# A graph network on one core: rows turned by transposing DMAs in the batch norm stage, and the middle attention stage's transfers cut by subtile

## The chip, the cores and the metric

The kernel runs on 1 core of one Trainium2 chip. The metric is the device time of one execution in microseconds (us). TensorE multiplies, VectorE, ScalarE and GpSimd do the elementwise work, and SyncE issues most DMAs; the engines meet only at semaphores.

## The reference

Four graph layers stand one behind the other, each with a residual and a layer norm, on 10,000 nodes with 512 features and 5,000 edges:

```
x = layernorm(x + L0(x))   # GIN: two products with W1, W2
x = layernorm(x + L1(x))   # SAGE: two products, batch norm, relu, + x
x = layernorm(x + L2(x))   # GAT twice (4 heads of 256), then a product with Wfc
x = layernorm(x + L3(x))   # GCN: product, batch norm, gelu, + x
```

What matters here: the last step of layer 1, `relu((h - mu) * rsqrt(var + eps) * gamma + beta) + x`, then `layernorm(x + ...)`, then the first product of layer 2, `x @ W1` (512 to 1024 columns), with 8 more columns for the attention logits. And the middle of layer 2: the output of the first attention, relu, times `W2` (1024 to 1024, with 8 logit columns).

## The kernel before, in words

The nodes are padded to 20 groups of 512 (G = 20; GROUP), each of 4 subtiles of 128 rows (S = 4). In the code a group g is named by its pair i and its parity u, g = 2i + u; most buffers are double, by parity. The layers are cut into stages, run one after the other; at a stage's end all engines meet. Within a stage each engine has its own program, in an order that is written out by hand, and waits on semaphores. `in_pairs` runs a body over all groups, `following(i, u)` is the next group, `ahead(i, G)` says that a pair i + 1 exists. Two stages are touched.

Products. fp32 values are split into a high and a low fp16 part, and each product is three fp16 matmuls per chunk of 128 (`split_product`, lines 324 to 326). The rows' parts are the stationary operand, so they are needed with the features on the partitions: turned against the row layout in which norms are computed. 1032 output columns are worked in three thirds of 344.

Batch norm stage (`batch_norm_stage`, from line 1886, "sage"). SyncE loads h (features on partitions) and x (rows on partitions), 1 MB each per group (lines 1937, 1941). ScalarE applies scale, shift and relu to h (2036). TensorE turns h into rows with fp32 transposes against an identity, 4 per subtile (`turn_rows`, 2080). VectorE adds 2x (`residual`, 1997) and takes statistics (1432, 1435), GpSimd the power (1441, 1444), VectorE normalises into b_o (`finish`, 1452). TensorE turns b_o back (`turn_back`, 2090), 4 chunks of 4 transposes into two PSUM banks; ScalarE takes the high parts from PSUM (2042) and VectorE the low parts (2011). Then come the products, 12 of 12 matmuls for a group (`products`), ScalarE copies each third to b_wide (2057), SyncE stores 516 KB per subtile to h1 (1958). GpSimd adds a bias to b_o (1973), SyncE stores it (1948). Everything for group g+1 is worked while TensorE is at the products of g: its group is two blocks of eight transposes for turn_rows and two for turn_back, set between the products.

Middle attention stage (`gat_middle_stage`, from line 2130). For each subtile SyncE loads rows of h1 (512 KB, line 2182), GpSimd gathers sums (1463), VectorE mixes both into t_z (2250) and adds a bias (2255), ScalarE takes relu (2268) and casts the high part t_row_hi (2271), GpSimd the low part t_row_lo (2224). Here the rows are turned by DMAs, not by TensorE: `turn(g)` on SyncE issues one transposing DMA of 128x4096 fp16 for the high parts of a whole group (2190) and one for the low parts (2193), each after all four subtiles are there. Both go through single row buffers, which are free for group g+1 when the transfers of g have landed. TensorE does 288 matmuls per group, ScalarE copies the thirds (2282), SyncE stores (2198).

All the DMAs of SyncE go through one queue, in the order of its program; the first stage of the kernel turns rows by DMA as well (1518, 1521), 128x2048 at a time.

Of the kernel before, what the change touches and what calls it, by code (L numbers as in the profile page):

```python
# [11 lines left out]
ds = bass.ds  # L12
# [118 lines left out]
def in_pairs(eng, n, body):  # L131

    if n > 2:
        with eng.Fori(0, n // 2 - 1) as i:
            for u in range(2):
                body(i, u, False)
    body(n // 2 - 1, 0, False)
    body(n // 2 - 1, 1, True)
# [1750 lines left out]
def batch_norm_stage(kn, layer):  # L1889
# [17 lines left out]
    if sage:  # L1907
        z_hi = kn.buffer(mem, "b_z_hi", [P, 2, 4, D], F16)
        z_lo = kn.buffer(mem, "b_z_lo", [P, 2, 4, D], F16)
        wide = two("b_wide", [P, GAT_ROW], F32)  # L1910
    norm = Norm(kn, mem)

    tp = [[kn.bank[n] for n in (0, 1, 0, 1)]] * 2 if sage else [kn.bank[0:4], kn.bank[4:8]]
    tq = [kn.bank[2], kn.bank[3]]
# [10 lines left out]
    turned = pair("turned", 4 * H if sage else 0)  # L1925
    hi_done = take("hi_done", 4 * G if sage else 0)
    lo_done = take("lo_done", 4 * G if sage else 0)
    prod = take("prod", THIRDS * S * G if sage else 0)
    wide_done = take("wide_done", THIRDS * S * G if sage else 0)
    wide_stored = pair("wide_stored", 16 * 2 * G if sage else 0)  # L1930

    def sync(sp):
        def load(i, u):

            sp.wait_ge(rows_turned[u].sem, rows_turned[u].at(i * S))
            settle(sp, kn)
            sp.dma_start(h[u][:], dram["h"][:, :, ds(i * (2 * GROUP) + u * GROUP, GROUP)]
                         .rearrange("m p n -> p m n")).then_inc(h_in[u].sem, 16)

            sp.wait_ge(y_done[u].sem, y_done[u].at(i * S))  # L1940
            sp.dma_start(x[u][:], node_rows(x_dram, i, u)).then_inc(x_in[u].sem, 16)

        def store(i, u):
            if sage:
                sp.wait_ge(biased[u].sem, biased[u].at(i + 1))
            else:
                sp.wait_ge(rows_out[u].sem, rows_out[u].at(i * S + S))
            sp.dma_start(node_rows(out_dram, i, u), o[u][:]).then_inc(stored[u].sem, 16)

        def group(i, u, last):  # L1950
            g = i * 2 + u
            if ahead(i, G):
                load(i + 1, u)
            store(i, u)
            if sage:
                for s in range(S):
                    sp.wait_ge(wide_done.sem, wide_done.at((g * S + s + 1) * THIRDS))
                    sp.dma_start(dram["h1"][ds(i * (2 * GROUP) + u * GROUP + s * P, P), :], wide[s % 2][:])\
                        .then_inc(wide_stored[s % 2].sem, 16)

        load(0, 0)
        load(0, 1)
        in_pairs(sp, G, group)
        for u in range(2):
            sp.wait_ge(stored[u].sem, stored[u].at(16 * H))
            if sage:
                sp.wait_ge(wide_stored[u].sem, wide_stored[u].at(16 * 2 * G))

    def gpsimd(pool):
        def bias(i, u):  # L1970

            pool.wait_ge(turned[u].sem, turned[u].at(i * 4 + 4))
            nc.gpsimd.tensor_tensor(o[u][:], o[u][:], kn.fc_b[:].unsqueeze(1).broadcast_to([P, S, D]), ALU.add)\
                .then_inc(biased[u].sem, 1)

        def group(i, u, last):
            if not last:
                norm.pool(pool, *following(i, u))
                bias(*following(i, u))

        if sage:
            norm.pool(pool, 0, 0)
            bias(0, 0)
# [4 lines left out]
    def vector(dve):  # L1988
# [18 lines left out]
        def low_parts(i, u):  # L2007
            g = i * 2 + u
            for k in range(4):
                dve.wait_ge(hi_done.sem, hi_done.at(g * 4 + k + 1))  # L2010
                v.scalar_tensor_tensor(out=z_lo[:, u, k, :], in0=tq[k % 2][:], scalar=A_SCALE, in1=z_hi[:, u, k, :],
                                       op0=ALU.mult, op1=ALU.subtract).then_inc(lo_done.sem, 1)

        def group(i, u, last):
            if not last:
                residual(*following(i, u), range(S))
                finish(*following(i, u))
                low_parts(*following(i, u))
# [7 lines left out]
        residual(0, 0, range(S))  # L2026
        if sage:
            finish(0, 0)
            low_parts(0, 0)
        in_pairs(dve, G, group if sage else group_alone)  # L2030

    def scalar(act):
# [6 lines left out]
        def high_parts(i, u, chunks=range(4)):  # L2039
            for k in chunks:  # L2040
                act.wait_ge(turned[u].sem, turned[u].at(i * 4 + k + 1))
                act.activation(z_hi[:, u, k, :], tq[k % 2][:], ACT.Copy, scale=A_SCALE).then_inc(hi_done.sem, 1)

        def group(i, u, last):
            g = i * 2 + u
            for s in range(S):

                if s == 1 and ahead(i, G):
                    apply(i + 1, u)

                w = wide_stored[s % 2]
                act.wait_ge(w.sem, w.at(g * 32 + (s // 2) * 16))
                for n in range(THIRDS):
                    if (s, n) in ((2, 2), (3, 1)) and not last:
                        high_parts(*following(i, u), (0, 1) if s == 2 else (2, 3))
                    act.wait_ge(prod.sem, prod.at((g * S + s) * THIRDS + n + 1))
                    act.activation(wide[s % 2][:, n * THIRD:(n + 1) * THIRD], mm[n], ACT.Copy, scale=UNSCALE)\
                       .then_inc(wide_done.sem, 1)

        if sage:  # L2060
# [3 lines left out]
            in_pairs(act, G, group)  # L2064
# [3 lines left out]
    def tensor(pe):  # L2068
        def turn_rows(i, u, subtiles):
            pe.wait_ge(f_done[u].sem, f_done[u].at(i * 4 + 4))  # L2070
            for s in subtiles:

                if not sage:
                    pe.wait_ge(y_done[u].sem, y_done[u].at((i - 1) * S + s + 1))
                elif s >= 2:
                    pe.wait_ge(y_done[u].sem, y_done[u].at(i * S + s - 1))
                else:
                    pe.wait_ge(y_done[1 - u].sem, y_done[1 - u].at((i + u) * S))
# [4 lines left out]
        def turn_back(i, u, chunks=range(4)):  # L2083
            g = i * 2 + u
            pe.wait_ge(rows_out[u].sem, rows_out[u].at(i * S + S))
            for k in chunks:

                pe.wait_ge(lo_done.sem, lo_done.at(g * 4 + (k - 1 if k >= 2 else 0)))
                for s in range(S):
                    ins = pe.transpose(tq[k % 2][:, s * P:(s + 1) * P], o[u][:, s, k * P:(k + 1) * P], kn.ident[:])  # L2090
                ins.then_inc(turned[u].sem, 1)

        def products(i, u, s, thirds=range(THIRDS)):
            g = i * 2 + u
            parts = lambda k: (z_hi[:, u, k, s * P:(s + 1) * P], z_lo[:, u, k, s * P:(s + 1) * P])
            for n in thirds:
# [6 lines left out]
        def group(i, u, last):  # L2103
            pe.wait_ge(lo_done.sem, lo_done.at((i * 2 + u) * 4 + 4))
            if not last:
                turn_rows(*following(i, u), (0, 1))
            products(i, u, 0)
            if not last:
                turn_rows(*following(i, u), (2, 3))
            products(i, u, 1)  # L2110
            products(i, u, 2, (0, 1))
            if not last:
                turn_back(*following(i, u), (0, 1))
            products(i, u, 2, (2,))
            products(i, u, 3, (0,))
            if not last:
                turn_back(*following(i, u), (2, 3))
            products(i, u, 3, (1, 2))

        if sage:  # L2120
            turn_rows(0, 0, range(S))
            turn_back(0, 0)
# [8 lines left out]
def gat_middle_stage(kn):  # L2131
# [39 lines left out]
    turned_in = pair("turned_in", 32 * H)  # L2171
# [4 lines left out]
    def sync(sp):  # L2176
        def load_rows(g):
            for s in range(S):
                if g:
                    i, u = divmod(g - 1, 2)  # L2180
                    sp.wait_ge(z_mixed.sem, z_mixed.at((g - 1) * S + s + 1))
                sp.dma_start(hrow[:, s, :], dram["h1"][g * GROUP + s * P:g * GROUP + (s + 1) * P, LOGITS:])\
                    .then_inc(h_in[s].sem, 16)

        def turn(g):
            i, u = divmod(g, 2)
            if g >= 2:
                sp.wait_ge(prod.sem, prod.at((g - 1) * S * THIRDS))
            sp.wait_ge(hi_done.sem, hi_done.at(g * S + S))
            sp.dma_start(r_hi[u][:], row_hi[:].rearrange("p s c -> p (s c)"), transpose=True)\  # L2190
                .then_inc(turned_in[u].sem, 16)
            sp.wait_ge(lo_done.sem, lo_done.at(g * S + S))
            sp.dma_start(r_lo[u], row_lo[:].rearrange("p s c -> p (s c)"), transpose=True)\
                .then_inc(turned_in[u].sem, 16)
# [5 lines left out]

        load_rows(0)
        load_rows(1)
        turn(0)
        load_rows(2)
# [11 lines left out]
    def gpsimd(pool):  # L2216

        def low_parts(g):
            i, u = divmod(g, 2)
            if g:  # L2220
                pool.wait_ge(turned_in[1 - u].sem, turned_in[1 - u].at((i + u) * 32))
            for s in range(S):
                pool.wait_ge(hi_done.sem, hi_done.at(g * S + s + 1))
# [39 lines left out]
    def scalar(act):  # L2263
        def parts(i, u, s):
# [4 lines left out]
            act.wait_ge(turned_in[1 - u].sem, turned_in[1 - u].at((i + u) * 32))  # L2269
# [23 lines left out]
    def tensor(pe):  # L2293
        def group(i, u, last):
            g = i * 2 + u
            pe.wait_ge(turned_in[u].sem, turned_in[u].at(i * 32 + 32))
            for s in range(S):
                for third in range(THIRDS):
# [608 lines left out]
```

## Time and profile before

| | |
|---|---|
| median of 3 runs | 4138.68 us (4137.36 to 4145.64) |
| the profiled execution | 4137.12 us, span 4135.1 us |
| TensorE busy | 3554.7 us, 86% |
| VectorE, ScalarE, GpSimd busy | 2089.7, 1479.1, 1476.6 us |
| DMA | 800.08 MB, mean 193 GB/s |
| batch norm stage | about 1317 to 1833 us of the span |
| middle attention stage | about 2020 to 2912 us |

Busy time is the time in which an engine has an instruction under way. "Clock" is the share of TensorE's full clock that was granted; DMA share is the mean busy share of the core's 16 DMA engines, and can pass 1 when packets overlap.

### The profile page before, as it was taken

The numbers are of one execution on the slowest core, as the hardware profiler recorded it, in microseconds if no ns is written. First come the engines' busy times: TensorE is split into PE (matmuls) and PEld (weight loads), VectorE is DVE, ScalarE is ACT, GpSimd is POOL, SyncE is SP. The second block draws the span as 40 slices with busy tenths as digits, with TensorE's granted clock in tenths as the row PEclk, the third lists the DMA queues.
The fourth block names the chain that finished last, engine by engine and source line by source line (L and its number), as shares of the span: only waits on it lengthen the run. The fifth ranks groups of instructions, "written<-read, shape, count | busy, mean of one in ns | idle before, by whom it ended". The sixth has DMA issues, their size and how long they took to land. (4 is left out here: it accounts for less than half of the span.)

```text
span 4135.1 us, 57582 instructions
## 1 busy us (share of the span) xinstructions
PE 3554.7 (86%) x20056; PEld 2138.1 (52%) x20056; DVE 2089.7 (51%) x3927; ACT 1479.1 (36%) x2584; POOL 1476.6 (36%) x1231
## 2 busy tenths in 40 slices
PE   4589994499997999988399999999777999948974
PEld 3134441255553777766266666666554555514543
DVE  7167775523332444437644343330566878605668
ACT  1333332322222444435233233332343344343357
POOL 2445543332221222235333333230436666434312
PEclk7789997699998999999699999999998999989985
DMA  1667776633343566549686766763777776466548
GB/s 67 211 181 198 199 183 203 214 127 129 122 131 113 194 220 217 209 168 279 203 229 198 202 201 200 207 176 89 211 216 265 264 265 254 163 216 201 176 162 276
DMA packets 533322, 800.08 MB, mean 193 GB/s; under 512 B 287494, under 2 KB 287494, under 8 KB 531152
## 3 DMA queue, kind: packets, MB, share of 16 engines
q1 hardware_dynamic: 466000, 577.37, 42.7%
q0 software_dynamic: 67200, 221.25, 18.5%
q8 instruction: 57, 0.93, 0.1%
q14 instruction: 65, 0.53, 0.0%
HBM read 470.83 MB, written 263.59 MB: 178 GB/s over the span
## 5 line engine op out<-in xcount | busy, mean ns | idle before, releaser
L325 PE MATMUL bank<-w_lo,t_r_hi 128*128 128x344 f16 (+1 forms) x2560 | 837.3, 327 | 0.0
L326 PE MATMUL bank<-w_hi,t_r_hi 128*128 128x344 f16 (+1 forms) x2560 | 837.1, 327 | 0.0
L324 PE MATMUL bank<-w_hi,w_lo 128*128 128x344 f16 (+1 forms) x1280 | 419.2, 327 | 30.9 <-DMA w_lo<-g_row_lo 30.9
L2250 DVE SCALAR_TENSOR_TENSOR t_z<-w_lo,t_z 128x256 f32<-128x256 f32 x320 | 209.2, 714 | 441.2 <-DMA w_lo<-h 438.5
L2224 POOL TENSOR_TENSOR t_row_lo<-t_r,t_row_hi 128x1024 f16<-128x1024 f32 x80 | 184.6, 2308 | 513.2 <-ACT t_row_hi L2271 513.0
L324 PE MATMUL bank<-l_z_hi,w_lo 128*128 128x512 f16 x960 | 364.4, 380 | 1.4 <-DVE l_z_lo L2633 1.4
L325 PE MATMUL bank<-l_z_lo,w_hi 128*128 128x512 f16 x960 | 364.3, 379 | 0.0
L326 PE MATMUL bank<-l_z_hi,w_hi 128*128 128x512 f16 x960 | 364.1, 379 | 0.0
L1463 POOL DMA_INDIRECT l_z<-sum,slot_i x160 | 165.9, 1037 | 484.1 <-PE bank L1833 284.8
L326 PEld LDWEIGHTS bank<-w_hi,t_r_hi 128*128 128x128 f16 x2560 | 250.9, 98 | 168.6 <-issue 0.8
L324 PE MATMUL bank<-w_hi 128*128 128x344 f16 x960 | 297.5, 310 | 45.8 <-DMA w_hi<-t_row_lo 45.8
L325 PEld LDWEIGHTS bank<-w_lo,t_r_hi 128*128 128x128 f16 x2560 | 250.9, 98 | 162.3 <-issue 0.6
L324 PE MATMUL bank<-w_hi,b_z_lo 128*128 128x344 f16 x960 | 296.6, 309 | 0.0
L325 PE MATMUL bank<-w_lo,b_z_hi 128*128 128x344 f16 x960 | 296.6, 309 | 0.0
L326 PE MATMUL bank<-w_hi,b_z_hi 128*128 128x344 f16 x960 | 296.6, 309 | 0.0
L2282 ACT ACTIVATE w_hi<-bank 128x344 f32<-128x344 f32 x240 | 109.3, 457 | 512.0 <-PE bank L326 512.0
L1063 PE MATMUL bank<-e_rows,e_lhs 128*128 128x512 f32 x240 | 159.2, 786 | 148.2 <-ACT e_out L1052 65.6
L324 PE MATMUL bank<-w_hi,t_r_lo 128*128 128x512 f16 x640 | 243.3, 380 | 0.0
L2426 POOL TENSOR_TENSOR t_r_lo<-t_r,t_r_hi 128x512 f16<-128x512 f32 x160 | 196.2, 1235 | 97.4 <-ACT t_r_hi L2494 91.1
L1792 DVE BATCH_NORM_STATS2 bn_stats<-l_h 128x512 f32 (+2 forms) x80 | 54.5, 682 | 337.2 <-ACT l_h L1814 299.6
L2491 ACT ACTIVATE t_r<-bank,vec_scaled 128x512 f32<-128x512 f32 x160 | 109.7, 685 | 293.3 <-PE bank L2522 241.6
L1463 POOL DMA_INDIRECT t_z<-sum_gat,slot_i x160 | 166.2, 1039 | 122.1 <-SPq L291 79.2
(332 smaller groups left out, 7005.6 us busy)
## 6 DMA issues: line engine op xcount, KB each, us to landing
w_lo<-h SPq DMA_DIRECT2D x160, 512.0 KB
h<-b_wide SPq DMA_DIRECT2D x80, 516.0 KB, 2.9
h<-w_hi SPq DMA_DIRECT2D x80, 516.0 KB, 3.2
sum_gat<-a_out SPq DMA_DIRECT2D x80, 514.0 KB
l_x<-x SPq DMA_DIRECT2D x40, 1024.0 KB
sum<-e_out SPq DMA_DIRECT2D x120, 256.0 KB
g_x<-in_x SPq DMA_DIRECT2D x20, 1024.0 KB
x<-g_y SPq DMA_DIRECT2D x20, 1024.0 KB
```

The lines of the kernel that those rows point to most:

```text
L324: pe.matmul(out, s_lo, m_hi, start=(k == 0), stop=False)
L325: pe.matmul(out, s_hi, m_lo, start=False, stop=False)
L326: mm = pe.matmul(out, s_hi, m_hi, start=False, stop=last)
L1063: pe.matmul(total[t % 2][:], lhs[t % L][:], rows[t % W][:], start=True, stop=True).then_inc(summed.sem, 1)
L1463: pool.indirect_dma_start(out, None, sums, bass.IndirectOffsetOnAxis(ap=kn.slot_i[:, g * S + s:g * S + s + 1], axis=0), bounds_check=kn.d. ...
L1792: v.bn_stats(kn.bn_stats[:, m, ds(g * 6, 6)], h[u][:, m, 0:real]).then_inc(seen.sem, 1)
L2224: nc.gpsimd.tensor_tensor(row_lo[:, s, :], r_f[s % 2][:], row_hi[:, s, :], ALU.subtract)\
L2250: ins = v.scalar_tensor_tensor(out=z[u][:, s, cols], in0=hrow[:, s, cols], scalar=z[u][:, s, HC + h:HC + h + 1], in1=z[u][:, s, cols], op0 ...
L2282: act.activation(wide[s % 2][:, third * THIRD:(third + 1) * THIRD], mm[s % 2][third], ACT.Copy, scale=UNSCALE).then_inc(wide_done.sem, 1)
L2426: g_.tensor_tensor(r_lo[:, u, k, :], r_f[k % 2][:], r_hi[:, u, k, :], ALU.subtract)\
L2491: act.activation(r_f[k % 2][:], tp[k % 4][:], ACT.Relu, scale=A_SCALE, bias=kn.vec_scaled[:, bias + k:bias + k + 1]).then_inc(r_done.sem, 1)
```

## The change

In the batch norm stage the normalised rows b_o are split in the row layout (ScalarE's `high_parts` and VectorE's `low_parts`, now from SBUF, by subtile) and turned by SyncE's DMAs, two of 128x512 fp16 per subtile, eight per group. `turn_back` is gone. The turned parts lie in the region of weights that are dead by then. The wide buffer is fourfold. TensorE turns the rows of group g+2 as one piece behind the first subtile's products of g, ScalarE's scale and shift runs three groups ahead, and SyncE's program is unrolled and reordered. In the middle stage the two transposing DMAs per group become eight of 128x1024, two per subtile, set between the row loads and the stores; the semaphores are by subtile.

```
-    tp = [[kn.bank[n] for n in (0, 1, 0, 1)]] * 2 if sage else ...
-    tq = [kn.bank[2], kn.bank[3]]
+    tp = [kn.bank[0:4]] * 2 if sage else [kn.bank[0:4], kn.bank[4:8]]
+    wide = [kn.buffer(mem, f"b_wide{s}", [P, GAT_ROW], F32) for s in range(S)]
...
 sync (batch norm)
+        def turn(g, s):
+            u = g % 2
+            if g >= 2:
+                sp.wait_ge(prod.sem, prod.at((g - 1) * S * THIRDS))
+            sp.wait_ge(turned_in[s].sem, turned_in[s].at(g * 32))
+            for rows, done, out in ((row_hi, hi_done, z_hi), (row_lo, lo_done, z_lo)):
+                sp.wait_ge(done.sem, done.at(g * S + s + 1))
+                sp.dma_start(out[u][:, s * 4:(s + 1) * 4, :], rows[:, s, :], transpose=True)\
+                    .then_inc(turned_in[s].sem, 16)
...
+        for g in range(2):
+            load_h(0, g)
+            load_x(0, g)
+        if sage:
+            for g in range(2, 4):
+                load_h(1, g - 2)
+                load_x(1, g - 2)
+            for s in range(S):
+                turn(0, s)
+            store(0, 0)
+            for g in range(G):
+                if g + 1 < G:
+                    for s in range(S):
+                        turn(g + 1, s)
+                store_wide(g, 0)
+                if g + 4 < G:
+                    load_h(*divmod(g + 4, 2))
+                if g + 1 < G:
+                    store(*divmod(g + 1, 2))
+                store_wide(g, 1)
+                if g + 4 < G:
+                    load_x(*divmod(g + 4, 2))
+                store_wide(g, 2)
+                store_wide(g, 3)
...
 gpsimd: the bias waits for lo_done of the group, not for turned
 vector: group is residual(i, u), finish(i, u), low_parts(i, u) of its own group
+            for s in range(S):
+                dve.wait_ge(hi_done.sem, hi_done.at(g * S + s + 1))
+                dve.wait_ge(turned_in[s].sem, turned_in[s].at(g * 32))
+                v.scalar_tensor_tensor(out=row_lo[:, s, :], in0=o[u][:, s, :], scalar=A_SCALE, in1=row_hi[:, s, :],
...
 scalar
+                if s == 1 and ahead(i, G) and (u == 0 or ahead(i + 1, G)):
+                    apply(*following(i + 1, u))
+                if s == 3 and ahead(i, G):
+                    high_parts(i + 1, u)
...
             apply(0, 0)
             apply(0, 1)
             high_parts(0, 0)
+            apply(1, 0)
+            high_parts(0, 1)
...
 tensor
         def group(i, u, last):
+            products(i, u, 0)
+            if ahead(i, G):
+                turn_rows(i + 1, u, range(S))
+            for s in range(1, S):
+                products(i, u, s)
...
             turn_rows(0, 0, range(S))
-            turn_back(0, 0)
+            turn_rows(0, 1, range(S))
```

And the middle stage, on SyncE:

```
+        for s in range(S):
+            load_rows(0, s)
+        for s in range(S):
+            load_rows(1, s)
+            turn(0, s)
+        for s in range(S):
+            load_rows(2, s)
         for g in range(G):
-            if g + 1 < G:
-                turn(g + 1)
-            store_wide(g, 0)
-            if g + 3 < G:
-                load_rows(g + 3)
-            for s in range(1, S):
+            for s in range(S):
+                if g + 1 < G:
+                    turn(g + 1, s)
+                if g + 3 < G:
+                    load_rows(g + 3, s)
                 store_wide(g, s)
```

`turn(g, s)` is here as in the batch norm stage, with 8 chunks per subtile; TensorE waits for a subtile's two transfers ahead of its products, and ScalarE's casts and GpSimd's low parts wait for the transfers of the same subtile of the group before.

## Rows read from the trace of the kernel before

**Rows 1.** Windows: busy us (count) by engine, clock, DMA share, GB/s.
```profile
1374.26:1496.72 122.46, 122.46 (x882) 88.54 (x881) 53.04 (x101) 51.81 (x100) 28.81 (x15) 1.00 0.60 215
2115.55:2829.50 713.95, 713.95 (x4898) 479.01 (x4896) 245.88 (x322) 226.92 (x340) 218.92 (x128) 1.00 0.68 193
```

**Rows 2.** TensorE's waits: 1340 to 1829 us, then 1840 to 2900 us.
```profile
PE bank L2080 <- DVE b_z_lo L2011: 1.8, 1, 1.8
...
PE bank L324 <- DMA w_hi<-t_row_lo: 45.8, 1, 45.8
```

**Rows 3.** Timeline, SyncE's wide stores: start, us, instruction.
```profile
1374.26 18.70 SPq L1958 DMA_DIRECT2D h<-b_wide  x4
...
1496.72 18.70 SPq L1958 DMA_DIRECT2D h<-b_wide  x4
```

**Rows 4.** Timeline, TensorE around one block of eight transposes.
```profile
1505.38 0.31 PE L326 MATMUL bank<-w_hi,b_z_hi 128*128 128x344 f16 x1
1505.52 1.04 PE L2090 MATMUL bank<-ident,b_o 128*128 128x128 f32 x8
1506.39 0.31 PE L324 MATMUL bank<-w_hi,b_z_lo 128*128 128x344 f16 x1
```

**Rows 5.** Groups by line, TensorE, 1343.7 to 1829.5 us: busy, mean ns, idle before.
```profile
L2090 PE MATMUL bank<-ident,b_o 128*128 128x128 f32 x304 | 39.4, 273 | 0.0
```

**Rows 6.** Groups by line, five groups' time, 1374.26 to 1496.72 us.
```profile
L1973 POOL TENSOR_TENSOR b_o<-b_o,fc_b 128x2048 f32<-128x2048 f32 x5 | 22.7, 4544 | 48.4 <-PE bank L2090 48.4
...
L1997 DVE SCALAR_TENSOR_TENSOR b_y<-b_x,bank 128x512 f32<-128x512 f32 x21 | 14.5, 688 | 27.9 <-PE bank L2080 27.9
L1432 DVE BATCH_NORM_STATS2 n_stats<-b_y 128x6 f32<-128x512 f32 x20 | 13.9, 695 | 0.7
L2011 DVE SCALAR_TENSOR_TENSOR b_z_lo<-bank,b_z_hi 128x512 f16<-128x512 f32 x20 | 12.9, 686 | 33.0 <-ACT b_z_hi L2042 33.0
...
L1452 DVE TENSOR_SCALAR b_o<-b_y,n_moments,n_power 128x512 f32<-128x512 f32 x20 | 9.6, 543 | 7.1 <-POOL n_power L1444 7.1
```

**Rows 7.** Transposing DMAs by tile: ns on SyncE's queue, min/median/max; a landing time.
```profile
L1518 SPq DMA_TRANSPOSE w_hi<-g_row_hi x20: 1757/2187/3123, 218.3 to 621.3; - x20
...
L2193 SPq DMA_TRANSPOSE w_hi<-t_row_lo x10: 4884/4917/17132, 2051.3 to 2793.3; - x10
...
DMA to landing us min/median/max: 6.7/6.8/19.2
```

**Rows 8.** Timeline, start of the batch norm stage, VectorE and TensorE.
```profile
1334.95 1.91 DVE L1452 TENSOR_SCALAR b_o<-b_y,n_moments,n_power 128x512 f32<-128x512 f32 x4 [1.55 <-POOL n_power L1444]
...
1343.69 0.31 PE L324 MATMUL bank<-w_hi,b_z_lo 128*128 128x344 f16 x1
```

**Rows 9.** Timeline, TensorE's second and fourteenth matmul of the middle stage.
```profile
2070.87 0.49 PE L325 MATMUL bank<-w_lo,t_r_hi 128*128 128x344 f16 x1
...
2074.31 0.32 PE L325 MATMUL bank<-w_lo,t_r_hi 128*128 128x344 f16 x1
```

**Rows 10.** Timelines, start of the middle stage: ScalarE, GpSimd, SyncE, VectorE, TensorE.
```profile
2033.03 1.05 ACT L2271 CAST t_row_hi<-t_r 128x1024 f16<-128x1024 f32 x1
...
2034.16 2.47 POOL L2224 TENSOR_TENSOR t_row_lo<-t_r,t_row_hi 128x1024 f16<-128x1024 f32 x1 [3.47 <-ACT t_row_hi L2271]
...
2046.36 2.35 POOL L2224 TENSOR_TENSOR t_row_lo<-t_r,t_row_hi 128x1024 f16<-128x1024 f32 x1 [0.31 <-ACT t_row_hi L2271]
...
2051.28 17.13 SPq L2193 DMA_TRANSPOSE w_hi<-t_row_lo  x1
2068.46 2.00 SPq L2182 DMA_DIRECT2D w_lo<-h  x4
...
2049.42 1.22 DVE L2255 TENSOR_TENSOR t_z<-t_z,w_hi 128x1024 f32<-128x1024 f32 x1
...
2057.95 1.22 DVE L2255 TENSOR_TENSOR t_z<-t_z,w_hi 128x1024 f32<-128x1024 f32 x1
2072.48 8.41 DVE L2250 SCALAR_TENSOR_TENSOR t_z<-w_lo,t_z 128x256 f32<-128x256 f32 x4 [13.31 <-DMA w_lo<-h]
...
2070.61 0.46 PE L324 MATMUL bank<-w_hi 128*128 128x344 f16 x1 [45.82 <-DMA w_hi<-t_row_lo]
```

More of the change, by code:

```diff
@@ L128, in settle, with in_pairs @@
     eng.sem_inc(kn.passed, 1)
-def in_pairs(eng, n, body):
-    if n > 2:
-        with eng.Fori(0, n // 2 - 1) as i:
+def in_pairs(eng, n, body, apart=1):
+    if n > 2 * apart:
+        with eng.Fori(0, n // 2 - apart) as i:
             for u in range(2):
                 body(i, u, False)
-    body(n // 2 - 1, 0, False)
-    body(n // 2 - 1, 1, True)
+    for i in range(n // 2 - apart, n // 2):
+        body(i, 0, False)
+        body(i, 1, i == n // 2 - 1)
 def ahead(i, n):
@@ L1907, in batch_norm_stage @@
     if sage:
-        z_hi = kn.buffer(mem, "b_z_hi", [P, 2, 4, D], F16)
-        z_lo = kn.buffer(mem, "b_z_lo", [P, 2, 4, D], F16)
-        wide = two("b_wide", [P, GAT_ROW], F32)
+        row_hi = kn.buffer(mem, "b_row_hi", [P, S, D], F16)
+        row_lo = kn.buffer(mem, "b_row_lo", [P, S, D], F16)
+        dead = [w[:, 0:2 * S * 4 * P].rearrange("p (u a n) -> p u a n", u=2, n=P) for w in (kn.w_hi, kn.w_lo)]
+        z_hi, z_lo = ([w[:, u] for u in range(2)] for w in dead)
+        wide = [kn.buffer(mem, f"b_wide{s}", [P, GAT_ROW], F32) for s in range(S)]
     norm = Norm(kn, mem)
-    tp = [[kn.bank[n] for n in (0, 1, 0, 1)]] * 2 if sage else [kn.bank[0:4], kn.bank[4:8]]
-    tq = [kn.bank[2], kn.bank[3]]
+    tp = [kn.bank[0:4]] * 2 if sage else [kn.bank[0:4], kn.bank[4:8]]
     mm = [kn.bank[4 + n][:, 0:THIRD] for n in range(THIRDS)]
@@ L1950, in group, with store_wide @@
         def group(i, u, last):
-            g = i * 2 + u
             if ahead(i, G):
-                load(i + 1, u)
+                load_h(i + 1, u)
+                load_x(i + 1, u)
             store(i, u)
[L1955 to L1963, printed above, removed]
+        def store_wide(g, s):
+            sp.wait_ge(wide_done.sem, wide_done.at((g * S + s + 1) * THIRDS))
+            sp.dma_start(dram["h1"][g * GROUP + s * P:g * GROUP + (s + 1) * P, :], wide[s][:])\
+                .then_inc(wide_stored[s].sem, 16)
+        for g in range(2):
[22 more added lines that the diff above has]
+                store_wide(g, 3)
+        else:
+            in_pairs(sp, G, group)
         for u in range(2):
             sp.wait_ge(stored[u].sem, stored[u].at(16 * H))
-            if sage:
-                sp.wait_ge(wide_stored[u].sem, wide_stored[u].at(16 * 2 * G))
+        if sage:
+            for s in range(S):
+                sp.wait_ge(wide_stored[s].sem, wide_stored[s].at(16 * G))
     def gpsimd(pool):
         def bias(i, u):
-            pool.wait_ge(turned[u].sem, turned[u].at(i * 4 + 4))
+            pool.wait_ge(lo_done.sem, lo_done.at((i * 2 + u) * S + S))
             nc.gpsimd.tensor_tensor(o[u][:], o[u][:], kn.fc_b[:].unsqueeze(1).broadcast_to([P, S, D]), ALU.add)\
@@ L1976, in group @@
         def group(i, u, last):
-            if not last:
-                norm.pool(pool, *following(i, u))
-                bias(*following(i, u))
+            norm.pool(pool, i, u)
+            bias(i, u)
         if sage:
-            norm.pool(pool, 0, 0)
-            bias(0, 0)
             in_pairs(pool, G, group)
@@ L2008, in low_parts @@
             g = i * 2 + u
-            for k in range(4):
-                dve.wait_ge(hi_done.sem, hi_done.at(g * 4 + k + 1))
-                v.scalar_tensor_tensor(out=z_lo[:, u, k, :], in0=tq[k % 2][:], scalar=A_SCALE, in1=z_hi[:, u, k, :],
+            for s in range(S):
+                dve.wait_ge(hi_done.sem, hi_done.at(g * S + s + 1))
+                dve.wait_ge(turned_in[s].sem, turned_in[s].at(g * 32))
+                v.scalar_tensor_tensor(out=row_lo[:, s, :], in0=o[u][:, s, :], scalar=A_SCALE, in1=row_hi[:, s, :],
                                        op0=ALU.mult, op1=ALU.subtract).then_inc(lo_done.sem, 1)
         def group(i, u, last):
[L2015 to L2018, printed above, removed]
+            residual(i, u, range(S))
+            finish(i, u)
+            low_parts(i, u)
         def group_alone(i, u, last):
@@ L2024, in group_alone @@
             finish(i, u)
-        residual(0, 0, range(S))
         if sage:
-            finish(0, 0)
-            low_parts(0, 0)
-        in_pairs(dve, G, group if sage else group_alone)
+            in_pairs(dve, G, group)
+        else:
+            residual(0, 0, range(S))
+            in_pairs(dve, G, group_alone)
     def scalar(act):
@@ L2071, in turn_rows @@
             for s in subtiles:
-                if not sage:
+                if sage:
+                    pe.wait_ge(y_done[1 - u].sem, y_done[1 - u].at((i + u - 1) * S + s + 1))
+                else:
                     pe.wait_ge(y_done[u].sem, y_done[u].at((i - 1) * S + s + 1))
[L2075 to L2078, printed above, removed]
                 for m in range(4):
@@ L2081, in turn_rows, with products @@
                 ins.then_inc(rows_turned[u].sem, 1)
-        def turn_back(i, u, chunks=range(4)):
+        def products(i, u, s):
             g = i * 2 + u
[L2085 to L2096, printed above, removed]
+            parts = lambda k: (z_hi[u][:, s * 4 + k, :], z_lo[u][:, s * 4 + k, :])
+            pe.wait_ge(turned_in[s].sem, turned_in[s].at(g * 32 + 32))
+            for n in range(THIRDS):
                 pe.wait_ge(wide_done.sem, wide_done.at((g * S + s - 1) * THIRDS + n + 1))
@@ L2176, in sync, with load_rows, turn @@
     def sync(sp):
[L2177 to L2186, printed above, removed]
+        def load_rows(g, s):
+            if g:
+                sp.wait_ge(z_mixed.sem, z_mixed.at((g - 1) * S + s + 1))
+            sp.dma_start(hrow[:, s, :], dram["h1"][g * GROUP + s * P:g * GROUP + (s + 1) * P, LOGITS:])\
+                .then_inc(h_in[s].sem, 16)
+        def turn(g, s):
+            u = g % 2
             if g >= 2:
                 sp.wait_ge(prod.sem, prod.at((g - 1) * S * THIRDS))
[L2189 to L2194, printed above, removed]
+            sp.wait_ge(turned_in[s].sem, turned_in[s].at(g * 32))
+            for rows, done, out in ((row_hi, hi_done, r_hi), (row_lo, lo_done, r_lo)):
+                sp.wait_ge(done.sem, done.at(g * S + s + 1))
+                sp.dma_start(out[u][:, s * CH:(s + 1) * CH, :], rows[:, s, :], transpose=True)\
+                    .then_inc(turned_in[s].sem, 16)
         def store_wide(g, s):
```

60 lines of the change are left out of this document (20 added, 40 removed).

## The prediction

> **What bounds the kernel now.** I read the busy shares first, then the windows of the two stages that the diff touches, then who waits for whom on TensorE, then the timelines of each stage's start. In the steady part of the batch norm stage TensorE is busy for the whole window at a granted clock of 1.00 (the 2.4 GHz level), while VectorE, ScalarE and GpSimd stand at 43%, 42% and 24% and the DMA share is 0.60; in the steady part of the middle attention stage it is the same picture with a DMA share of 0.68 [rows 1]. TensorE's waits agree: from 1340 to 1829 us it waits once, for 1.8 us, and in the whole middle stage it has one large wait, 45.8 us, at the start, for the transposed low parts of group 0 [rows 2]. So in both stages only two things can save time: work taken off TensorE, and an earlier first product.
>
> **Batch norm, steady part.** The period of a group is (1496.72 - 1374.26) / 5 = 24.49 us, from the first wide store of one group to that of the group five later [rows 3]. Four blocks of eight fp32 transposes stand in each group. One costs the step from the product ahead of it to the product behind it less an ordinary step: 1506.39 - 1505.38 - 0.145 = 0.87 us [rows 4]. So the 144 products take 24.49 - 4 x 0.87 = 21.0 us. The change takes out the two blocks that turn the rows back: in the stream of products they are 304 matmuls, 16 in each of 19 groups [rows 5], so 19 x 2 x 0.87 = 33.1 us. The new order also has 18 and not 19 pairs of row-turning blocks between the products (group 1 is turned before them): 1.7 us more. Sum 34.8 us off the stream; the new period is 22.7 us.
>
> Does anything else need more than 22.7 us? VectorE has four residuals, four statistics, four normalisations and four low parts, at 688, 695, 543 and 686 ns [rows 6], some 10.6 us with the aggregates, and no longer waits on PSUM copies of its own input. In TensorE's group g (time from its start) the rows of g+2 are turned at 5.3 to 7.0; residual and statistics take 4 x 1.65, to about 12.3; GpSimd's power 1.4; normalisation to 15.9. ScalarE reaches its high parts (s = 3) at about 18, and they end at about 20.5, VectorE's low parts a microsecond later. The eight transposing DMAs of g+1 wait for the end of group g-1's products, are issued from about 0.9, and are wanted by ScalarE at 18 and by TensorE at 22.7: over 10 us of cover. The bias addition, 4544 ns [rows 6], now waits for the low parts, not for the transposes; its store comes behind the load of h in the next group, and its buffer is wanted a period later. Four wide buffers in place of two give each store a full period. In SyncE's new list nothing is queued ahead of a transfer that becomes ready later than it by more than some microseconds.
>
> The cost that the trace doesn't show is a transposing DMA of 128x512. The nearest rows: 128x2048 (512 KB) holds the queue 1.76 to 3.12 us, median 2.19, and 128x4096 (1 MB) 4.88 us and more, landing 6.8 us after issue, 1.9 behind the issue's end [rows 7]. The larger transfer costs 2.8 times the smaller at the minimum, so no fixed part is to be seen, and I take the time as proportional: 1 MB per group is 4.9 us, 0.61 for each of eight. Ends: 0.44 (a quarter of 1.76) and 1.76 (no cheaper for being smaller). The DMA engines now work 0.60 x 24.49 = 14.7 us per group [rows 1, 3]; with 4.9 that is 19.6 us of 22.7, a share of 0.86. The cover is thin: it lasts until a piece costs (22.7 - 14.7) / 8 = 1.0 us.
>
> The Trainium skill speaks against cutting transfers up: DMA: Bandwidth & Descriptors, section Rules for kernel authors, wants many small transfers joined, and its table Measured has 64 KB in 0.95 us and 1 MB in 6.15. By a straight line between these a piece of 128 KB would be estimated at 1.3 us, eight at 10.4, and the DMA work at 25.1 us a group, over the present period. The rows above point the other way, since the 512 KB transfers are cheaper by the byte than the 1 MB ones.
>
> **Batch norm, start.** Before, group 0's rows are normalised from 1334.95 and the first product starts at 1343.69, already at the full clock, because transposes ran just ahead [rows 8]. After, low parts of group 0 follow the normalisation: 1336.9 + 4 x 0.69 = 1339.6. But SyncE issues the transposes of group 0 behind the load of x for group 3, which waits until VectorE has made all four residuals of group 1, and these stand behind the low parts: 1339.6 + 3 x 1.65 + 0.69 = 1345.3. The load itself (1 MB, some 3 us of the DMA engines at the 215 GB/s at share 0.60 of [rows 1]), two transposing pieces (1.2) and the 1.9 of landing give a first product at about 1351.8, 8 us later than before. TensorE will have been idle since about 1334 and starts at the 1.2 GHz level: in the middle stage twelve steps after such a gap take 3.44 us, 0.287 each against 0.145, so 1.7 us is lost [rows 9]. The start costs 10 us; ends 4 (transposes overtake the load of x) and 16. Nothing changes at the stage's end. Batch norm: 34.8 - 10 = 25 us gained.
>
> **Middle stage, start.** SyncE before turns group 0 in two transfers after all four subtiles: the low one is issued at 2051.28, holds the queue 17.13 us while gathers and other transfers fill the engines, and products start at 2070.61; but subtile 0's high part is cast from 2033.03 and its low part runs from 2034.16 for 2.47 us [rows 10]. After, subtile 0's two pieces (128x1024, 1.2 us each by proportion) are issued by 2036.7 and land at about 2040. Subtile 1 is there 3 us later. Subtile 3's low part starts at 2046.36 [rows 10] and ends at 2048.7; with 3.1 us it is there at 2052, when TensorE, taking 10.5 us per subtile, is still at subtile 0 or 1. So the first product moves by 30 us, the cold start stays as it is. What could be late next: ScalarE stands in order, and its high part of group 2, subtile 0 comes ahead of group 0's fourth copy; VectorE began that subtile at 2072.48, after rows whose loads were issued only at 2068.46 behind the long low transfer [rows 10]. These loads now go out as VectorE has mixed each subtile of group 1, 2049.4 to 2058.0 by the starts of its bias additions [rows 10], so the subtile should be ready near 2064; TensorE stalls only if it is later than about 2073. I take 28 of the 30 us; ends 12 and 31.
>
> **Middle stage, steady part.** TensorE's work is unchanged. Transposes of group g+1 go out as the stores of group g do, the last at about 32 us of a period of 42.0, and are wanted 10 us later for subtile 0 (which went first) and 41 us later for subtile 3. ScalarE may wait 1 to 5 us for a row buffer at subtiles 2 and 3; six PSUM banks cover this. DMA work is 0.68 x 42 = 28.6 us. I count nothing, either way.
>
> **Sum.** 25 + 28 = 53 us. The profiled execution took 4137.1 us (span 4135.1), so it would take 4084; the median of the runs is 1.6 us above it: 4086.
>
> **Rivals.**
> (a) The middle stage's start gives only part: gathers and row loads of groups 1 and 2 keep the engines full (the low transfer took 17.13 us there [rows 10]), ScalarE sits on group 2, TensorE stalls. Gain 25 + 12 = 37 or less: about 4106 (4098 to 4116). Against it: the traffic is the same and merely begins earlier.
> (b) The DMA engines bind in batch norm, mildly. At 1.1 us a piece the period is 14.7 + 8.8 = 23.5; 19 x 0.8 = 15 us are lost: 4101.
> (c) The same at 1.25 to 1.35 us a piece, where the skill's table would put it: 25.1 x 20 = 502 against 485.5 before, with the start's 10 the stage loses 27 and the middle stage's 28 cancel it: 4138, no change.
> (d) Slower. A transposing piece has a mostly fixed price. At 1.76 us, the shortest row of 128x2048, DMA work is 28.8 us a group; the stage takes 576 + 10 against 485.5, loses 100, and the total is 4138.7 + 100 - 28 = 4211. It decides from 1.3 us a piece. For it: no row shows a piece this small. Against it: the comparison of 512 KB and 1 MB.
>
> **How the numbers follow.** About 0.2% (8 us) is what a measurement can tell from no change. Forecast 0.70, (a) 0.11, (b) 0.07, (c) 0.04, (d) 0.08. Faster 0.88, same 0.04, slower 0.08. The forecast's own range by its ends: fastest 34.8 - 4 + 31 = 62 us, 4077; slowest 34.8 - 16 + 20, 4100. The range runs from 4070 to 4118, so that it holds (a) and (b) too and leaves out (c), (d) and a little beyond.
>
> **What would show it.** Batch norm's period 22.7 us (first wide store to first wide store) at TensorE busy 100%, clock 1.00, no transpose of b_o, DMA share about 0.86. First product of that stage about 8 us later from the stage's start, with some twelve slow ones. In the middle stage the wait for the first transposed part 15 us and not 46, then no gap over 1 us. Wrong if: TensorE shows waits for transposing DMAs in the steady batch norm stage, pieces over 1.0 us each, or a stall between products 30 and 70 us into the middle stage.

## The result, and the profile after

The changed kernel runs in 4098.17 us (median of 4, 4089.31 to 4100.99) against 4138.02; the ratio is 0.9898 with a 95% interval of 0.9876 to 0.9919, or 42 us less by the ratio (34 to 51) and 40 by the medians. Forecast were 53 us less, 4086, in a range of 4070 to 4118. The profiled execution has a span of 4099.3 us against 4135.1, 36 us less; it is the slowest of the four.

First, the waits of TensorE in the changed kernel: the batch norm stage from its second group of matmuls on, where nothing is listed at all; then, for 1300 to 3000 us (line, releaser, us in total, times, longest), the starts of the two stages and the one new wait. They answer to [rows 2].

```profile
PE bank L325 <- DMA w_hi<-t_row_lo: 17.9, 1, 17.9
PE bank L325 <- DMA w_lo<-b_row_lo: 17.3, 1, 17.3
PE bank L325 <- ACT w_hi L2297: 9.0, 2, 6.1
```

The wait of 45.8 us at the start of the middle stage is 17.9. But 9.0 us are new: TensorE waits for ScalarE's copies of finished products (L2297), which no row of before shows.

The windows of the two steady parts (columns as in [rows 1]):

```profile
1413.84:1773.00 359.16, 359.16 (x2525) 250.11 (x2524) 158.18 (x304) 157.66 (x311) 90.58 (x46) 1.00 0.90 270
2115.00:2800.00 685.00, 685.00 (x4699) 459.61 (x4698) 265.70 (x305) 210.19 (x327) 202.19 (x125) 1.00 0.82 193
```

TensorE is busy throughout at clock 1.00 in both. The DMA share went from 0.60 to 0.90 in the first and from 0.68 to 0.82 in the second, there with the same 193 GB/s. What takes the engines longer for the same bytes there is not shown: the pieces are smaller and also stand in another order, and in the batch norm stage the size of the pieces hardly moves the share (e5, below).

From one train of eight pieces on SyncE's queue in batch norm (start, us on the queue); it begins at 1738.01, and the last line is the store behind it. Below, the window of that train, columns as above:

```profile
1739.38 1.26 SPq L1954 DMA_TRANSPOSE w_lo<-b_row_lo  x1
1740.75 1.20 SPq L1954 DMA_TRANSPOSE w_hi<-b_row_hi  x1
...
1748.55 0.58 SPq L1972 DMA_DIRECT2D h<-b_wide  x1
```
```profile
1738.01:1748.50 10.49, 10.49 (x78) 7.64 (x77) 5.04 (x11) 2.29 (x5) 1.94 (x1) 1.00 0.58 138
```

A piece of 128x512 costs 1.20 us (high parts) and 1.27 us (low parts) at the median on the queue, twice the 0.61 of the forecast, and this train 10.5 us. Single pieces take up to 5.9 us, so other trains are longer.

The span of both executions, cut at the first or last instruction of a kind. The last column is the change of the stretch; stages marked as untouched are not in the diff:

| stretch | before | after | change |
|---|---|---|---|
| up to the batch norm coefficients (untouched) | 1312.6 | 1310.0 | -2.6 |
| coefficients to the last copy to b_wide | 516.8 | 491.8 | -25.0 |
| first attention stage (untouched) | 191.2 | 193.3 | +2.1 |
| middle stage: first gather to first product | 50.0 | 22.2 | -27.8 |
| middle stage: first product to the next stage's first gather | 846.0 | 857.8 | +11.8 |
| the rest (untouched) | 1218.5 | 1224.3 | +5.8 |

### The profile page after: what moved, and what is told of

Same layout as the page of the kernel before. It is cut to its first block and busy times, and to the rows that moved or that the text cites. A ratio compares the mean times of both kernels' runs of the same rounds, so it can differ in the third digit from the quotient of the medians.

```text
span 4099.3 us, 57066 instructions
## 1 busy us (share of the span) xinstructions
PE 3529.6 (86%) x19736; PEld 2108.2 (51%) x19736; DVE 2115.1 (52%) x3927; ACT 1467.8 (36%) x2584; POOL 1457.7 (36%) x1231
## 5 line engine op out<-in xcount | busy, mean ns | idle before, releaser
L325 PE MATMUL bank<-w_hi,w_lo 128*128 128x344 f16 (+1 forms) x2240 | 716.0, 320 | 48.6 <-DMA w_lo<-g_row_lo 31.3
L2265 DVE SCALAR_TENSOR_TENSOR t_z<-w_lo,t_z 128x256 f32<-128x256 f32 x320 | 238.3, 803 | 405.8 <-DMA w_lo<-h 402.5
L326 PE MATMUL bank<-w_lo,w_hi 128*128 128x344 f16 (+1 forms) x1280 | 419.2, 328 | 0.0
L327 PE MATMUL bank<-w_hi 128*128 128x344 f16 (+1 forms) x1280 | 419.2, 328 | 0.0
L2239 POOL TENSOR_TENSOR t_row_lo<-t_r,t_row_hi 128x1024 f16<-128x1024 f32 x80 | 175.3, 2192 | 513.4 <-ACT t_row_hi L2286 513.4
L325 PE MATMUL bank<-w_hi 128*128 128x344 f16 x960 | 298.5, 311 | 27.0 <-DMA w_hi<-t_row_lo 17.9
L325 PEld LDWEIGHTS bank<-w_hi,w_lo 128*128 128x128 f16 x2240 | 219.5, 98 | 180.1 <-issue 51.4
L2297 ACT ACTIVATE w_hi<-bank 128x344 f32<-128x344 f32 x240 | 104.5, 454 | 333.3 <-PE bank L327 317.9
```

Of the source, the lines that this page charges most:

```text
L325: pe.matmul(out, s_lo, m_hi, start=(k == 0), stop=False)
L326: pe.matmul(out, s_hi, m_lo, start=False, stop=False)
L327: mm = pe.matmul(out, s_hi, m_hi, start=False, stop=last)
L2239: nc.gpsimd.tensor_tensor(row_lo[:, s, :], r_f[s % 2][:], row_hi[:, s, :], ALU.subtract)\
L2265: ins = v.scalar_tensor_tensor(out=z[u][:, s, cols], in0=hrow[:, s, cols], scalar=z[u][:, s, HC + h:HC + h + 1], in1=z[u][:, s, cols], op0 ...
L2297: act.activation(wide[s % 2][:, third * THIRD:(third + 1) * THIRD], mm[s % 2][third], ACT.Copy, scale=UNSCALE).then_inc(wide_done.sem, 1)
```

## Experiments

The same cuts for all profiled executions, in us; "ratio" is over the timed runs against the kernel before:

| kernel | up to bn | bn | first attention | mid start | mid body | rest | ratio (95%) |
|---|---|---|---|---|---|---|---|
| e0_after | 1307.6 | 493.3 | 192.2 | 21.7 | 853.8 | 1221.1 | 0.9895 (0.9879 to 0.9912) |
| e1_bn_only | 1308.8 | 493.2 | 192.6 | 50.5 | 846.5 | 1223.4 | 0.9950 (0.9938 to 0.9963) |
| e2_mid_only | 1307.9 | 518.8 | 190.8 | 21.5 | 854.6 | 1222.4 | 0.9945 (0.9932 to 0.9959) |
| e3_mid_turn1 | 1311.5 | 493.4 | 192.5 | 21.5 | 861.2 | 1223.6 | 0.9886 (0.9871 to 0.9900) |
| e4_bn_start | 1303.5 | 483.2 | 192.2 | 21.7 | 858.2 | 1223.5 | 0.9883 (0.9868 to 0.9897) |
| e5_bn_whole | 1303.9 | 496.6 | 191.8 | 22.1 | 851.2 | 1223.1 | 0.9892 (0.9876 to 0.9909) |
| e6_bn_halves | 1311.2 | 636.0 | 190.1 | 21.9 | 850.4 | 1227.1 | 1.0242 (1.0223 to 1.0262) |
| e8_act_order | 1306.3 | 483.3 | 192.0 | 21.7 | 845.6 | 1218.5 | 0.9862 (0.9845 to 0.9878) |
| e9_act_only | 1310.1 | 493.3 | 192.2 | 21.8 | 845.7 | 1222.0 | 0.9868 (0.9852 to 0.9884) |
| e4_again | 1310.6 | 483.9 | 191.8 | 22.7 | 850.7 | 1222.8 | 0.9861 (0.9842 to 0.9879) |
| e8_again | 1311.6 | 483.8 | 192.4 | 21.9 | 846.9 | 1224.1 | 0.9858 (0.9841 to 0.9874) |

### Each half alone: e1_bn_only, e2_mid_only

```
e1: batch_norm_stage as changed, gat_middle_stage as before
e2: batch_norm_stage as before, gat_middle_stage as changed
```

> Only the batch norm stage is changed, the middle stage is as before. Theory (TensorE binds the stage; 35 us of transposes go, the later and colder start takes 10 back): stage 25 us shorter, total 25 us under before, 4113 us. No TensorE wait between the first product and the last; first product about 8 us later from the stage's start. Rival 1 (the 13 us that the whole change misses of its forecast were lost in this stage or in the stages behind it): only 12 to 18 us under before. Rival 2 (they were lost in the middle stage's start): 25, as the theory.

> Only the middle attention stage is changed. Theory: the first product comes 28 us earlier, and 9 us go to two stalls of TensorE in its first group, behind ScalarE's copies, which sit behind a cast that waits for a transposing DMA of group 1: 19 us under before, 4119 us. Rival (the stalls come from the earlier batch norm stage's other placement of buffers, or are chance): no stall, 28 us under before, 4110 us.

e1 took 4120.68 us against 4141.6 on that chip, 21 us less (15 to 26), and its stage is 23.6 us shorter: the theory's size, a little under. e2 took 4117.37, 24 us less (17 to 28); its start gained 28.5 us, its body lost 8.6, and TensorE waited for ScalarE with the old batch norm stage ahead of it too:

```profile
PE bank L324 <- ACT w_hi L2280: 5.7, 2, 5.4
```

So the two halves add up to the whole (21 + 24 against 42), and the stalls belong to the middle stage's own start. The rival that blamed the new batch norm stage falls.

### e3_mid_turn1: SyncE's order in the middle stage's start

```
         for s in range(S):
             load_rows(2, s)
+            turn(1, s)
         for g in range(G):
             for s in range(S):
-                if g + 1 < G:
+                if 0 < g and g + 1 < G:
                     turn(g + 1, s)
```

> The changed kernel with one more reordering: in the middle stage's start SyncE issues the transposes of group 1 right behind the row loads of group 2, subtile by subtile, and not between the stores of group 0. Theory (the stalls are SyncE's order: the transfer of group 1, subtile 1 is ready at about 18 us after the first product and issued 15 us later, behind a row load and a store): stalls of 9 us shrink to 0 to 3, total 6 to 9 us under the changed kernel, about 4090 us. Rival (the DMA engines are full there, whatever the order; the transfers of 7 and 9.5 us on the queue show it): the stalls stay at 6 to 12 us, total the same as the changed kernel, 4098 us.

The rival was right. The body is no shorter (861.2), TensorE's two stalls are 4.45 and 7.38 us, and the first transfer of group 1, issued 7.5 us earlier (9.1 if counted from the first product), stands on the queue longer, 12.69 us against 7.12. The rows, of e3's SyncE and then TensorE timeline:

```profile
2030.51 12.69 SPq L2207 DMA_TRANSPOSE t_r_hi<-t_row_hi  x1
...
2045.87 0.47 PE L325 MATMUL bank<-w_hi 128*128 128x344 f16 x1 [4.45 <-ACT w_hi L2298]
```

The DMA engines are full here (share 1.08 from 2020 to 2035 us in the changed kernel and 1.10 from there to 2040), and order on SyncE alone buys nothing.

### e4_bn_start, e4_again: the load that held the transposes back

```
-            for g in range(2, 4):
-                load_h(1, g - 2)
-                load_x(1, g - 2)
+            load_h(1, 0)
+            load_x(1, 0)
+            load_h(1, 1)
             for s in range(S):
                 turn(0, s)
+            load_x(1, 1)
```

> The changed kernel with the batch norm stage's load of x for group 3 moved behind the transposes of group 0 on SyncE. Theory (SyncE's wait for VectorE's residuals of group 1 holds the transposes back): first product 9 to 11 us earlier, total 9 to 11 us under the changed kernel, 4088 us. Rival (the start is given back: group 1's parts or the DMA engines, at 0.90 in this stage, are late next and TensorE then waits): first product earlier, but gaps behind it, total 0 to 4 us under.

> e4_bn_start once more, beside the two others on one chip. By the spans of the stages so far: 8.7 us under the changed kernel, 4085 to 4090.

In the changed kernel, SyncE and then TensorE (VectorE's fourth residual of group 1 ends at 1342.1, and the load goes out at once):

```profile
1342.14 0.37 SPq L1945 DMA_DIRECT2D b_x<-x  x1
1342.60 1.24 SPq L1954 DMA_TRANSPOSE w_hi<-b_row_hi  x1
...
1348.92 0.46 PE L325 MATMUL bank<-w_hi,w_lo 128*128 128x344 f16 x1 [17.33 <-DMA w_lo<-b_row_lo]
```

and TensorE in e4:

```profile
1332.53 0.47 PE L325 MATMUL bank<-w_hi,w_lo 128*128 128x344 f16 x1 [8.58 <-DMA w_lo<-b_row_lo]
```

From the stage's first instruction the first product comes after 38.9 us in the changed kernel (1310.0 to 1348.9) and 29.0 in e4 (1303.5 to 1332.5). The stage takes 483.2 and 483.9 us in the two executions of e4 against 491.8 and 493.3 in those of the changed kernel, 8 to 10 us less, and TensorE has no wait behind its first product. The total follows: 4088.39 and 4082.92 us. By their ratios to the kernel before that is 5 and 14 us under e0_after, too far apart for a closer figure.

### e5_bn_whole, e6_bn_halves: what a transposing piece costs

```
e5, turn(g), for the whole group, two DMAs:
+            if s:
+                return
...
-                sp.dma_start(out[u][:, s * 4:(s + 1) * 4, :], rows[:, s, :], transpose=True)
+                sp.dma_start(out[u], rows[:].rearrange("p s c -> p (s c)"), transpose=True)
e6, sixteen DMAs:
+                for n in range(2):
+                    sp.dma_start(out[u][:, s * 4 + n * 2:s * 4 + n * 2 + 2, :],
+                                 rows[:, s, n * 2 * P:(n + 1) * 2 * P], transpose=True)
```

> The changed kernel, but in the batch norm stage the transposing DMAs are two of 128x2048 per group and not eight of 128x512. Theory (a transposing DMA has a large fixed price: eight pieces hold the queue 10.3 us, two large ones 4 to 5): the DMA share of the stage falls from 0.90 towards 0.75 to 0.85 and stores are issued on time, but TensorE was bound already, so the total is the same as the changed kernel within 5 us, about 4098. Rival (the price goes by bytes, and pieces and whole cost the same): share stays at 0.90, queue time 10 us, total the same.

> The changed kernel, but in the batch norm stage each transposing DMA is cut in two: sixteen of 128x256 per group. Theory (mostly fixed price, about 1.2 us each): the pieces hold the queue 19 us a group, and with the plain transfers the DMA side needs 28 to 33 us against TensorE's 22.6: TensorE waits in the steady stage, total 100 to 200 us longer, 4200 to 4300. Rival (price by bytes, 0.6 us each): queue time stays at 10 us, total the same, 4098.

Times on the queue by tile, e5 and then e6:

```profile
L1956 SPq DMA_TRANSPOSE w_hi<-b_row_hi x20: 1957/3247/5417, 1336.5 to 1759.4; - x20
L1956 SPq DMA_TRANSPOSE w_lo<-b_row_lo x20: 1852/2022/2672, 1341.9 to 1762.7; - x20
```
```profile
L1955 SPq DMA_TRANSPOSE w_hi<-b_row_hi x160: 1167/1247/3411, 1343.7 to 1922.5; - x160
```

Half the size costs as much: 1.25 us for 128x256 at the median, 1.20 to 1.27 for 128x512; 128x2048 takes 1.85 at the least. So between these two small sizes the price on SyncE's queue does not move with the bytes. The period of e6, first store to first store, is 30.4 us; its queue has a DMA under way for 29.1 of them, 24.1 in the sixteen pieces, and TensorE waits:

```profile
1600.15 0.58 SPq L1973 DMA_DIRECT2D h<-b_wide  x1
...
1630.52 0.33 SPq L1973 DMA_DIRECT2D h<-b_wide  x1
```
```profile
PE bank L325 <- ACT b_wide L2094: 100.8, 20, 7.8
```
```profile
1450.00:1750.00 300.00, 248.54 (x1600) 165.23 (x1600) 105.72 (x200) 102.68 (x200) 57.23 (x30) 0.90 0.71 210
```

4238.19 us, 100 us over before: the slower case is one factor of two in the piece size away. In e6 the DMA share is only 0.71 (last window) while the queue is full, so it is the queue that binds there, not the engines. e5's total is that of the changed kernel (4092.90 against 4093.30 for e0 on the same chip), as TensorE binds in both; its DMA share in 1450 to 1750 us is 0.89, where I had expected 0.75 to 0.85. That part of the expectation failed: whole transfers are shorter on the queue (3.25 and 2.02 us at the median, 5.3 a group) but load the engines as much. They also start the stage later: TensorE's first wait is 22.0 us against 17.3 to 18.4 with pieces, and the stage 3 to 5 us longer.

### e8_act_order, e9_act_only, e8_again: ScalarE's order

```
+        def group(i, u, last, at=(3, 5, 7, 9), early=False):
             for n in range(THIRDS * S):
+                if early and n in (3, 4):
+                    parts(0, 1, n - 1)
-                if ahead(i, G) and n in (3, 5, 7, 9):
-                    parts(i + 1, u, (n - 3) // 2)
+                if ahead(i, G) and n in at:
+                    parts(i + 1, u, at.index(n))
...
+        group(0, 0, False, (8, 9, 10, 11), True)
+        group(0, 1, False)
```

Of group 1 only the first two subtiles are cast ahead of `group(0, 0, ...)`; the other two stand behind its third and fourth copy.

> The batch norm start of e4_bn_start, and in the middle stage's start ScalarE's order changed: group 0's first copies come ahead of group 1's last two casts, and group 2's casts stand behind its ninth to twelfth copy and not behind its third to ninth; later groups as before. SyncE's order is that of the changed kernel. Theory (TensorE's stalls are ScalarE standing at casts that wait for a transposing DMA, with finished products behind it; the full DMA engines only matter through that): stalls of 9 to 12 us and the cold clock behind them, 2.6 us, go; the stage's body falls to 846 to 849 us, total 9 to 12 us under e4_bn_start, about 4077. Rival (the DMA engines are behind, and group 1's parts or the stores would be late next): the body stays at 854 or more, total 4084 to 4090.

> ScalarE's order in the middle stage's start alone, on the changed kernel (batch norm stage as changed). Theory: the 4 to 12 us of stalls and the cold clock behind the longer of them go, nothing else moves: 6 to 12 us under the changed kernel, 4083 to 4090. Rival (it helped only because the batch norm start moved too, or by chance of that execution): within 3 us of the changed kernel, stalls of 4 us and more in the trace.

> e8_act_order once more. If the two edits add up: 15 to 20 us under the changed kernel and 6 to 12 us under e4_again, 4070 to 4081; if the stall's removal is given back elsewhere, the same as e4_again within 3 us.

ScalarE in the changed kernel, at the first stall (first line) and at the second:

```profile
2041.51 1.04 ACT L2286 CAST t_row_hi<-t_r 128x1024 f16<-128x1024 f32 x1 [1.60 <-DMA w_hi<-t_row_lo]
...
2047.91 1.06 ACT L2283 ACTIVATE t_r<-t_z 128x1024 f32<-128x1024 f32 x1 [4.31 <-DVE t_z L2270]
2058.28 1.04 ACT L2286 CAST t_row_hi<-t_r 128x1024 f16<-128x1024 f32 x1 [9.31 <-DMA w_lo<-t_row_lo]
```

All casts of group 1 stand ahead of the first copy in ScalarE's order; the last waits until 2041.51 for a transfer of group 0, and the copies come behind it. This is the first stall, of 2.9 us. Then ScalarE has the first rows of group 2 at 2047.91 and stands 9.31 us because the row buffer is not free until group 1's transfer has landed, with the copies that TensorE needs behind it again. TensorE's timeline at the same place:

```profile
2042.97 0.32 PE L325 MATMUL bank<-w_hi 128*128 128x344 f16 x1 [2.93 <-ACT w_hi L2297]
2059.74 0.47 PE L325 MATMUL bank<-w_hi 128*128 128x344 f16 x1 [6.10 <-ACT w_hi L2297]
...
2064.87 0.35 PE L325 MATMUL bank<-w_hi 128*128 128x344 f16 x1
```

After the 6.1 us the clock is at 1.2 GHz again: 18 steps take 5.13 us and not 2.6. Stalls of 9.0 and 2.5 us of slow clock are the 11.8 us of the table but for 0.3. With the copies ahead of the casts, in all three executions (e8, e9, e8_again) TensorE has no wait in the middle stage behind its first product, and the body is 845.6, 845.7 and 846.9 us, as before the change. By time e9 is at 4087.03 (ratio 0.9868), 11 us under the changed kernel by the ratios (0.9895 in e0; the two intervals overlap a little), but e8_again and e4_again, on one chip, do not differ (4082.84 and 4082.92), though the bodies are 846.9 and 850.7. So the expectation that the two edits add up to 6 to 12 us under e4_again failed. The stalls vary from one execution to the next (2.8 to 11.8 us in the eight executions with the changed middle stage and without the edit, bodies of 850.4 to 861.2), so what the edit is worth is 4 to 15 us in the trace of the stage, and the total does not resolve it in each comparison.

e8_act_order takes 0.9862 and 0.9858 of before, about 4082 us. By time it is not told apart from e4_again (0.9861).

### e0_after: the changed kernel again

> The changed kernel once more, for a comparison on the same chip as the three beside it, and to see how far the stages behind the changed ones move from one execution to the next. 4090 to 4101 us. If the 2 to 3 us by which the first attention stage is longer than before belong to the change, they are there again; if they are chance, not.

4093.30 us. The untouched stages behind the middle one take 1221.1 us here, 1224.3 in the first profile, 1218.5 both in the kernel before and in e8_act_order, and 1224.1 in e8_again. Its first attention stage is 192.2, and it is 190.1 to 193.3 over all kernels. With one profile of the kernel before, these 1 to 6 us can't be told from chance.

## Why the prediction was right, point by point

The measured 4098.17 us lie 12 us above the forecast and 8 below rival (a). Batch norm gave what was worked out for it. The middle stage gave 16.0 of the 28 us, by the mechanism of rival (a), and 13.3 to 23.7 in the other executions without e8's edit; with that edit it gave 27.2 to 28.7. The time is in the range because the range was drawn to hold (a) and (b). Two of the prediction's own signs of being wrong came: pieces over 1.0 us each, and stalls that end 48 and 65 us into the middle stage.

- **TensorE bounds both stages; 34.8 us leave the batch norm stream.** Right. Stream from first product to last copy: 485.7 us before, 452.9 after, 32.8 less, of which the cold clock took 1.3 (nine steps of 0.29 us).
- **Start of batch norm 10 us later.** Right: 31.1 us before, 38.9 after, plus the 1.3; by the very wait named, as e4 shows. The stage gained 25.0 us, forecast 25.
- **A transposing piece costs 0.61 us, by proportion.** Wrong by a factor of two on the queue: 1.20 to 1.27 us. Two rows of larger transfers [rows 7] were taken for a line through the origin, and e6 shows that the price below them does not fall with the bytes. That is where rivals (b) and (c) put the turning point, and by the prediction's own sum a group would have needed 14.7 + 9.9 = 24.6 us; yet the stage lost nothing. The reason is a second error, of the other sign: the sum set the queue time of the pieces beside the engines' time of the plain transfers, 0.60 x 24.49 us, and the bound of 1.0 us a piece followed. The two are separate budgets. In the train shown above the queue is full and the DMA share is 0.58 at 138 GB/s; at the start of another, just behind loads and stores (1419.57 to 1427.31 us), it is 1.03 at 384 GB/s, and the pieces hold the queue 3.7 and 3.9 us. The engines' own time for the pieces can be estimated, if the plain transfers cost what they did before: 0.90 x 22.7 - 14.7 = 5.7 us a group, 0.7 a piece, and in e6 0.71 x 30.4 - 14.7 = 6.9 us, 0.4 a piece. So 0.61 was about right for the engines and wrong for the queue. That the two errors cancelled is luck, not foresight. The reserve is small all the same. SyncE's first store of a group comes at 1413.84 and sixteen groups later at 1771.29, 22.3 us apart each, while TensorE needed 22.7: the queue ran behind from the stage's start and won back 0.4 us per group.
- **The Trainium skill's rule.** DMA: Bandwidth & Descriptors in the Trainium skill, section Rules for kernel authors, wants many small transfers joined. In e6, with pieces of 64 KB, going against it costs 145 us over e0_after; in e5 following it changes nothing in the total. By the table Measured of the same page of the Trainium skill the prediction's estimate was 1.3 us a piece. That table is for plain loads issued by GpSimd and counts the time of the DMA engines, while the 1.20 to 1.27 us are time on SyncE's queue and the engines' own time is estimated at 0.7, so the nearness of the two numbers does not bear the table out for this transfer.
- **Middle stage, first product 30 us earlier, 28 counted.** The shift was 27.8. The step that failed is "TensorE stalls only if it is later than about 2073": I had ScalarE wait for VectorE's mixing of group 2, and the mixing was in time. It waited for the row buffer, which a transposing DMA of group 1 held, with TensorE's copies behind it; and the casts of group 1, all ahead of the first copy, I had not asked about at all. I had counted such waits (1 to 5 us) as covered in the steady part and not asked in the start, where the engines are full. That is rival (a) at less than its price: 11.8 us back and not 16.
- **Steady middle stage: nothing.** Right: no wait of TensorE behind the first group in any run but e3, where the second stall (7.38 us) falls into the second group.
- **Sum.** 25.0 + 27.8 - 11.8 = 41 us in the touched stages, and 42 by the runs. The forecast's own slowest end, 4100, took 20 us for the middle stage's start where its stated end was 12; with 12 it is 4108, still in the range.

## What to carry to other kernels

When a start is pulled forward, look for instructions that stand in the same engine's order as the evacuation of results and wait for something that only the steady state delivers in time: here a cast that needed a buffer back from a DMA. Give issue time on a queue and busy time of the DMA engines each their own sum, and take the price of a small transfer from a transfer of that size. A load whose condition is late must not stand ahead of a transfer that is on the path (8 to 10 us, e4).

## What was not expected of the hardware

- Transposing DMAs of 128x256 and 128x512 fp16 hold SyncE's queue equally long, 1.25 and 1.20 to 1.27 us at the median; 128x2048 takes 1.85 us at the least in e5.
- The busy share of the DMA engines is nearly the same with two transposing DMAs per group (0.89 in e5) and with eight (0.90), though they hold the queue 5.3 and 10 us.
- With the middle stage's two transfers per group cut in eight and reordered the DMA share was 0.82 and not 0.68, at the same 193 GB/s; the cause is not shown.
- After a pause of TensorE of 6.1 us the granted clock was 1.2 and not 2.4 GHz for 18 matmul steps, and after the pause of 2.93 us 17 us before it was not. But in e5 a pause of 2.86 us was followed by ten steps at 1.2 GHz, so the length of the pause alone does not tell.
